# Opening rearranged, middle layers set up inside their own block, weight loads placed otherwise in the queue, last step's rows kept on chip

## The reference

```python
# 1: sliding-window attention (16 heads of 16, 4 key heads, window 64) and gelu feed-forward, 1024 wide
h = layernorm(x) * g1 + b1;  q, k, v = h @ Wq + bq, h @ Wk + bk, h @ Wv + bv;  q, k = rope(q), rope(k)
x = x + softmax(mask(q @ k.T / 4)) @ v @ Wo + bo
x = x + gelu((layernorm(x) * g2 + b2) @ Wf1 + bf1) @ Wf2 + bf2
# 2: two layers (8 heads of 64, windows of 128 and the window before)
for l in range(2):
    h = shift_token(x)                    # the right half of the columns comes from the row above
    q, k, v = split(h @ wqkv[l]);  q, k = xpos(l2norm(q) * qs[l]), xpos(l2norm(k) * ks[l])
    x = x + local_attention(8 * q, k, v) @ wo[l]
    h = layernorm(shift_token(x)) * lg[l] + lb[l]
    a, g = split(h @ w1[l] + b1[l]);  x = x + (a * gelu(g)) @ w2[l] + b2[l]
# 3: gated attention in chunks of 128: u * (relu(q @ k.T / sqrt(128) + bias)**2 @ v) @ o_w.T + o_b + x
# 4: linear layer with ternary weights
```

## Time and profile before

| | us |
|---|---|
| median of three runs (lowest, highest) | 2514.32 (2511.49, 2517.95) |
| the profiled execution's own time | 2506.83 |
| its span | 2505.0 |
| TensorE matmul busy | 2389.4 (95%) |
| VectorE busy | 1989.6 (79%) |
| ScalarE busy | 1570.0 (63%) |
| GpSimd busy | 1292.3 (52%) |

### The profile page before, as it was taken

One profiled execution on the slowest core, in us unless ns is written; L12 is line 12 of the kernel. 1 busy time (PEld: TensorE's weight loads), 2 busy tenths in 40 slices (PEclk: granted clock), 3 DMA queues, 4 the chain that ended last, 5 costly groups with the idle time before them and its releaser, 6 DMA issues. The chain is left out here.

```text
span 2505.0 us, 56134 instructions
## 1 busy us (share of the span) xinstructions
PE 2389.4 (95%) x19766; PEld 2160.8 (86%) x19766; DVE 1989.6 (79%) x6034; ACT 1570.0 (63%) x3630; POOL 1292.3 (52%) x1161
## 2 busy tenths in 40 slices
PE   7999999988899999999999999999879999999997
PEld 6899999977798998898888999999868888888886
DVE  6889989857889899899888999999567555775554
ACT  4788888755677887787777877877556113631111
POOL 3333233325766666767757667667247335743332
PEclk7999999997999999999999999999989999999998
DMA  2011221112222322323333223322343013311111
GB/s 80 21 34 38 71 86 59 35 43 82 91 82 89 98 82 87 98 85 111 105 102 98 89 80 98 92 77 92 100 155 107 28 34 101 97 59 34 34 34 43
DMA packets 223612, 189.75 MB, mean 76 GB/s; under 512 B 22372, under 2 KB 205800, under 8 KB 222312
## 3 DMA queue, kind: packets, MB, share of 16 engines
q1 hardware_dynamic: 204616, 176.52, 22.5%
q10 hardware_dynamic: 18720, 9.64, 1.4%
HBM read 90.60 MB, written 44.04 MB: 54 GB/s over the span
## 5 line engine op out<-in xcount | busy, mean ns | idle before, releaser
L1315 POOL TENSOR_TENSOR b_sb_probs<-b_sb_probs,b_sb_r_sum 128x512 f32<-128x512 f32 x256 | 269.3, 1072 | 330.8 <-DVE b_sb_r_sum L1568 330.8
L2078 POOL TENSOR_TENSOR c_kern_lo<-c_kern,c_kern_hi 128x512 fp32r<-128x512 f32 x128 | 178.2, 1392 | 302.3 <-ACT c_kern_hi L2167 302.3
L1399 ACT ACTIVATE b_sb_probs<-b_sb_probs,b_sb_neg_top,b_sb_r_norm 128x256 f32<-128x256 f32 x512 | 301.0, 590 | 2.1 <-DVE b_sb_neg_top L1535 1.2
L2167 ACT ACTIVATE c_kern_hi<-c_kern 128x512 fp32r<-128x512 f32 x128 | 80.9, 632 | 322.2 <-DVE c_kern L2277 322.2
L42 PE MATMUL psum<-b_sb_fT_lo,b_sb_w_hi 128*128 128x256 f32 x704 | 204.7, 291 | 1.4 <-DVE b_sb_fT_lo L1606 1.4
L42 PE MATMUL psum<-c_kern_lo,c_v_hi 128*128 128x512 f32 x512 | 199.7, 390 | 0.2
L44 PE MATMUL psum<-b_sb_fT_hi,b_sb_w_hi 128*128 128x256 f32 x704 | 199.6, 284 | 0.0
L44 PE MATMUL psum<-c_kern_hi,c_v_hi 128*128 128x512 f32 x512 | 199.5, 390 | 0.0
L43 PE MATMUL psum<-c_kern_hi,c_v_lo 128*128 128x512 f32 x512 | 199.3, 389 | 0.0
L43 PE MATMUL psum<-b_sb_fT_hi,b_sb_w_lo 128*128 128x256 f32 x704 | 199.3, 283 | 0.0
L1527 DVE CUSTOM_DVE_ANT_0 b_sb_probs<-psum,b_sb_mask 128x256 f32<-128x256 f32 x512 | 193.8, 416 | 2.1 <-PE psum L1712 1.6
(11 more groups left out here) (315 smaller groups left out, 8680.6 us busy)
## 6 DMA issues: line engine op xcount, KB each, us to landing
b_sb_kT_hi<-b_sb_kT_hi SPq DMA_DIRECT2D x64, 256.0 KB, 2.7
b_sb_kT_lo<-b_sb_kT_lo SPq DMA_DIRECT2D x64, 256.0 KB, 3.1
b_sb_v_prev<-b_sb_v_now SPq DMA_DIRECT2D x64, 256.0 KB, 2.5
Y<-b_sb_y SPq DMA_DIRECT2D x128, 128.0 KB, 2.5
b_sb_res<-Y SPq DMA_DIRECT2D x64, 128.0 KB, 2.9
b_sb_x_f<-Y SPq DMA_DIRECT2D x128, 64.0 KB, 2.1
b_sb_res_f<-Y SPq DMA_DIRECT2D x64, 128.0 KB, 2.5
U<-c_u_out SPq DMA_DIRECT2D x16, 512.0 KB, 4.6
```

What stands on the lines that cost most here:

```text
L1315: pool.tensor_tensor(p, p, r_sum[b][:, 2 * m:2 * m + 2, None].broadcast_to([P, 2, 2 * P]), ALU.mult)\
L1399: ins = act.activation(probs[b][:, n, :], probs[b][:, n, :], ACT.Exp, bias=neg_top[b][:, n:n + 1], scale=r_norm[b][:, h:h + 1], accum_out= ...
L2078: pool.tensor_tensor(kern_lo[i % RING][:], kern[i % RING][:], kern_hi[i % RING][:].bitcast(F32), ALU.subtract)\
L2167: act.activation(kern_hi[i % RING][:], kern[i % RING][:], ACT.Copy).then_inc(hi_ready, 1)
```

## The change

1. Opening of `layer_a`. The first row tile is loaded before the constants. The feed-forward weights leave `consts` for a part `weights_f` behind `load` 1. VectorE clears `qT` itself, with a semaphore of its own, and no engine waits for all constants at its start. In `project` the bias's matmul comes last and only it waits for the bias rows. `setup_a` is split: the weight's low part stays (`setup_w`), the bias rows move behind `norm` 1.
2. Passages. The last step's stores count on semaphores `a_handed` and `b_handed`, which live through the whole program. The end of the block does not wait for them; the next stage does, before its step 1 loads (SyncE and ScalarE in `layer_b`, SyncE in `layer_c`). They are cleared at the very end.
3. Opening of `layer_b`. The setup block is gone: its loads, splits and bias columns stand in the main lists, wqkv's parts first, w1's behind `turn_h` 1 and `spin_q` 0, wo's and w2's behind. The first six blocks of bias columns (`bias0`) are TensorE's first work, the other five come in step 0; the second layer's come in two pieces of five and six blocks, in steps 1 and 2 of TensorE's list, and `w1_early` is loaded after `rope` of step 1 and the splits. GpSimd clears fewer tiles, the keys' only in their left 128 columns.
4. `swap_f` 5 on SyncE moves from the ninth to the tenth shift and to the end of the turn.
5. In the last step `load_f` copies the rows from `y1` on chip, shifted by one partition for the right half, with the first row of that half from Y1.

```diff
 def layer_a(...):
-        "sp": [... ("load", 1, -1), ("consts", 0, -1),
+        "sp": [... ("load", 1, -1), ("weights_f", 0, -2), ("consts", 0, -1),
...
-                pool.memset(qT[b][:].bitcast(F32), 0.0).then_inc(consts_ready, 1)
...
-            dve.wait_ge(consts_ready, n_consts + 2)
+            for b in both:
+                dve.memset(qT[b][:].bitcast(F32), 0.0).then_inc(q_zeroed, 1)
...
-            pe.wait_ge(consts_ready, n_consts + 2)
...
             def project(t, b):
-                    pe.wait_ge(b_ready, 3)
+                    pe.wait_ge(consts_ready, n_consts + 2)
...
-                pe.matmul(out, e0[:], b_rows[:], start=True, stop=False)
                 for c in range(KC):
-                    ins = product3(..., False, c == KC - 1)
+                    product3(..., c == 0, False)
+                if t == 0:
+                    pe.wait_ge(b_ready, 3)
+                ins = pe.matmul(out, e0[:], b_rows[:], start=False, stop=True)
...
-            sp.wait_ge(y_stored, 16 * NT)
+            sp.wait_ge(y_stored, 16 * (NT - 1))
 def layer_b(...):
-        "pe": [... ("turn_p", 1, -1), ("bias", 0, 0), ("project_k", 1, 0), ...
+        "pe": [... ("down", 0, -4), ("bias", 2, -2), ..., ("up", 2, -3), ("bias", 1, -1), ..., ("project_v", 0, 0), ("bias", 0, 0), ...
-        "sp": [... ("down", 0, 8), ("swap_f", 5, 9), ("load_r", 0, 9), ... ("scores2", 0, 12)],
+        "sp": [... ("down", 0, 8), ("load_r", 0, 9), ... ("scores2", 0, 12), ("swap_f", 5, 10)],
...
-            setup = prepare.enter_context(nc.Block())
...
             def rope_(t, _):
                 if t == 1:
-                    sp.dma_start(w1_early[:], io["b2_w1"][1]).then_inc(early_in, 16)
+                    sp.wait_ge(a_handed, 32)
...
+                if t == 1:
+                    sp.wait_ge(raw_split, 7)
+                    ring.wait_full(sp, 0, ("bias", 0))
+                    sp.dma_start(w1_early[:], io["b2_w1"][1]).then_inc(early_in, 16)
...
             def load_f(t, b):
-                sp.wait_ge(stored[b], 16 * t + 16)
+                if t < steps - 1:
+                    sp.wait_ge(stored[b], 16 * t + 16)
...
+                if t == steps - 1:
+                    sp.wait_ge(stored[b], 16 * t)
+                    ring.wait_drained(sp, t, ("wo", b))
+                    sp.dma_start(x_f[:, b, 0:P], y1[b][:, 0:P]).then_inc(f_loaded[b], 16)
+                    sp.dma_start(x_f[1:P, b, P:D], y1[b][0:P - 1, P:D]).then_inc(f_loaded[b], 16)
+                    sp.dma_start(x_f[0:1, b, P:D], tile_rows(io["Y1"], t, b, slice(P, D), 1)[0:1, :]).then_inc(f_loaded[b], 16)
+                    return
...
         @block.scalar
+            for n in range(3):
+                act.activation(w_hi[:, :, qkv_cols(n)], w_raw0[:, :, qkv_cols(n)], ACT.Copy).then_inc(raw_hi, 1)
...
         @block.tensor
+            def shift(job, piece, cols, w, g):
+                out = ring.out(0, (job, piece), cols.stop - cols.start)
+                ring.wait_bank(pe, 0, (job, piece))
+                for n in range(cols.start, cols.stop):
+                    for c in range(KC):
+                        at = n - cols.start
+                        ins = pe.matmul(out[:, at:at + 1], w[:, c, n * P:(n + 1) * P], g[:, 1, c:c + 1], start=(c == 0),
+                                        stop=(c == KC - 1))
+                ring.written(0, ins, (job, piece))
+
+            shift("bias0", 0, slice(0, first), w1_raw0, gb)
...
+                    shift("bias", piece, early_cols[piece], w1_early, gb_next)
 def layer_c(...):
             def load(n):
+                if n == 1:
+                    sp.wait_ge(b_handed, 32)
```

More of the change, by code:

```diff
@@ L1076, in layer_b @@
         jobs.update(turn_f=["f"], up=["w"], down=["y"], bias=["bias"])
-        ring = Ring(sem, psum, f"{name}_ring", range(8), [(t, (job, b)) for stage, t, b in turns(order["pe"], steps)
+        ring = Ring(sem, psum, f"{name}_ring", range(8), [(0, ("bias0", 0))] + [(t, (job, b)) for stage, t, b in turns(order["pe"], steps)
                                                           if stage in jobs and (stage != "bias" or t == 0)
@@ L1267, in _ @@
                 sp.wait_ge(stored[b], 16 * steps)
-                sp.wait_ge(y2_stored[b], 16 * steps)
+                sp.wait_ge(y2_stored[b], 16 * (steps - 1))
         @block.gpsimd
         def _(pool):
-            pool.wait_ge(consts_ready, 9)
+            pool.memset(power[:], -0.5).then_inc(consts_ready, 1)
+            for b in both:
+                for part in (kT_hi[b], kT_lo[b]):
+                    pool.memset(part[:, :, 0:P].bitcast(F32), 0.0).then_inc(consts_ready, 1)
+                pool.memset(v_prev[b][:], 0.0).then_inc(consts_ready, 1)
+            pool.wait_ge(consts_ready, 7)
             def rope_(t, _):
+                if t == 0:
+                    pool.wait_ge(weights_in, 80)
                 pool.wait_ge(rope_loaded, 16 * t + 16)
@@ L1514, in spin_q, with add_bias @@
                 spin(t, b, 0, "q")
+                if (t, b) == (0, 0):
+                    for c in range(KC):
+                        dve.wait_ge(raw_hi, 4 + c)
+                        dve.scalar_tensor_tensor(out=w1_lo[:, c, :], in0=w1_raw0[:, c, :], scalar=gb[:, 0, c:c + 1],
+                                                 in1=w1_hi[:, c, :].bitcast(F32), op0=ALU.mult, op1=ALU.subtract)\
+                           .then_inc(raw_split, 1)
+            def add_bias(job, piece, out, of, n):
+                ring.wait_full(dve, 0, (job, piece))
+                ring.read(0, dve.tensor_tensor(out, ring.out(0, (job, piece), n), of, ALU.add), (job, piece))
+                ring.wait_drained(dve, 0, (job, piece))
             def turn_qk(t, b):
@@ L1629, in down, with bias @@
                 ring.read(t, dve.tensor_tensor(y2[:, b, :], ring.out(t, ("y", b), D), sum_f[:, b, :], ALU.add), ("y", b))
-            def bias(t, _):
-                if t == 0:
-                    ring.wait_full(dve, t, ("bias", 0))
-                    ring.read(t, dve.tensor_tensor(b1[:, 1, :], ring.out(t, ("bias", 0), n_in), b1[:, 1, :], ALU.add), ("bias", 0))
-                    ring.wait_drained(dve, t, ("bias", 0))
+            def bias(t, piece):
+                if t == 0 and piece == 0:
+                    dve.wait_ge(raw_hi, 6)
+                    dve.tensor_tensor(wo_lo[:], wo_raw0[:], wo_hi[:].bitcast(F32), ALU.subtract).then_inc(raw_split, 1)
+                    dve.wait_ge(raw_hi, 7)
+                    dve.tensor_tensor(w2_lo[:], w2_raw0[:], w2_hi[:].bitcast(F32), ALU.subtract).then_inc(raw_split, 1)
+                    add_bias("bias", 0, b1[:, 0, first:], b1_raw[:, first:], n_in - first)
+                    dve.sem_inc(bias_done, 1)
+                if t == 0 and piece > 0:
+                    dve.wait_ge(weights_in, 80)
+                    at = b1[:, 1, early_cols[piece]]
+                    add_bias("bias", piece, at, at, early_cols[piece].stop - early_cols[piece].start)
                     dve.sem_inc(early_done, 1)
```

205 lines of the change are left out of this document (97 added, 108 removed).

## The result

The changed kernel took 2507.58 us, median of 11 runs (2504.24 to 2513.38), against 2514.32 us of the kernel before (11 runs, 2511.16 to 2519.67): a ratio of 0.9972 with a 95% interval of 0.9961 to 0.9983, 6.7 us faster. The forecast was 12.2 us, 2502.1, in a range of 2489 to 2511. The profiled execution took 2505.77 us (span 2504.0, mean granted clock 0.973), only 1.1 us under that of before, which at 2506.83 was itself faster than all 11 runs.

What follows compares the result with a forecast made beforehand. TensorE was taken to bound the kernel, busy nearly everywhere at full clock, with gains only where it waits. Terms 3.9 + 1.7 + 3.5 + 0.7 + 1.0 + 1.4 = 12.2 us, from 2514.3 to 2502.1 us, range 2489 to 2511.

Steps and rivals of the forecast that it cites:

- Opening of the first stage: First stage's start: earlier normalisation, projection and second row tile, everything behind shifts; 3.9 us saved, between 1.5 and 4.5.
- The rival of the one-column matmuls: Bias groups inside dense work put TensorE at half clock, 13 us lost each: slower, 2541 us; chance 0.09.
- First passage: First to second stage: the block starts without waiting for the last store to land; 1.7 us saved, 1.6 to 2.0.
- Second passage: Passage to the last stage: SyncE goes on without waiting for the last store; 1.4 us saved, 1.2 to 1.6.
- Opening of the second stage: Second stage's start without setup block: earlier first scores, less clock and bias losses; net 3.5 us saved, 0 to 9.
- the 3.0 of the term: Second stage's first scores: loss set against the gain for TensorE at 1.2 GHz there, 3.0 us.
- The bias pieces: Second stage, steps 1 and 2: the next layer's 44 bias instructions as 20 and 24, 2.5 us taken as uncovered.
- Layer swap: Swap of layers: input weights issued a step earlier, so TensorE waits less; 0.7 us saved, 0 to 4.
- its upper case of 4 us: Layer swap: 4 us saved if the shorter gap also keeps the clock up.
- Last step: End of the second stage: rows copied on chip without waiting for the store; 1.0 us saved, 0 to 4.
- near 1790, and the term would be above 5: Last step: were the copy free of the queue, it would land in 1.7 us like a store.
- The rival "swallowed", 2506.5: Both stage openings: half of the 3.5 and 3.9 us comes back as VectorE's waits; 2506.5 us, chance 0.13.

Runs made afterwards that it cites:

- filler: Changed kernel plus twelve matmuls that compute nothing in TensorE's 2.15 us wait in the first stage's second step: 2486.4 us, 0.9976 of the kernel before.
- e_bopen: Kernel before with only the second stage's opening changed, the next layer's bias in two pieces included: 2495.3 us, ratio 1.0004.
- e_rows1: Kernel before with the last step's rows of the first sequence loaded ahead of the last stage's four early loads: 2487.1 us, ratio 0.9974.
- 2.7 in the second: Changed kernel timed again, unaltered, against the kernel before in a later session: 2491.6 us, ratio 0.9992.

## Why the prediction came out as it did

The direction and the range held in the first comparison; three steps were wrong, in size or sign, and a fourth, the layer swap, was sized too small. That the time still fell inside the range is in part luck.

*Opening of the first stage, 3.9 us.* Each step of the working came, and up to 53 us even 7.9 us, as the clock rose at 46.2 instead of 53.6. What I had not foreseen is that the clock then fell once more and took 7.2 us. What arrives at 115 us in the five traces of this opening without filler is 0.8, 0.5, 0.7, 5.2 and 5.0 us, 2.4 on average. The rival of the one-column matmuls named the kind of loss (a long stretch at half clock in a wholly busy engine) and the wrong cause: none of them stands at this place. That the 2.15 us wait starts it is likely and not shown: all six falls lie in it and none came where it was filled, but the traces with the filler differ from the others earlier. The Trainium skill (TensorE: Matmul & The Clock Gate, What's actually happening) says that activity releases the throttle: the traces with the filler agree, and the 20.5 us at half clock, without idle time behind the first 0.8 and spent on products of 17, 128 and 256 columns, do not. Why the old opening's equal wait passes in three traces of four stays open. (The new opening also holds a one-column copy on ScalarE, `warm`, that the description of the change leaves out; no run takes it alone.)

*First passage, 1.7 us:* 1.6. *Second passage, 1.4 us:* 1.1. Both by the next block beginning 2.1 us after the last issue.

*Opening of the second stage, 3.5 us.* The first failing step is in VectorE's chain. The first scores came 6.4 us earlier, not 7.7 to 9.0: they were forecast 27.0 us into the block and came at 29.6. VectorE's low parts of the weights were taken over at their price in the setup block, 3.3, 1.2 and 1.8 us. Here they stand in the main lists, beside GpSimd's work for keys and queries, and took 4.7, 1.6 and 2.6, which is 2.6 us more. (The 44 bias instructions, 9.3 us in the prediction, are 9.5 in the earlier trace rows; that hardly moves it.)

```profile
575.94 4.67 DVE L1519 SCALAR_TENSOR_TENSOR b_sb_w_lo<-b_raw_w,b_raw_gb,b_sb_w_hi 128x1408 fp32r<-128x1408 f32 x2
...
585.96 2.59 DVE L1650 TENSOR_TENSOR b_sb_w_lo<-b_raw_w,b_sb_w_hi 128x1536 fp32r<-128x1536 f32 x1
```

In all nine traces of the new opening they are longer, by 2.2 to 2.7 us together; why was not tried. The other two failing steps are those set against the gain. The clock was at half at the scores, as forecast, but filling the wait gives back some 1.2 us and not the 3.0 of the term. The bias pieces, of which I took 2.5 us as uncovered, cost their full 5.3 up to step 1's statistics: I had read "some 3 us to spare in each step" from a window that held TensorE's waits elsewhere in the step, and the groups stand where TensorE has none (idle for 0.0 us between 45 and 60 us into the block, and for 0.7 between 60 and 75). Kept at step 1's statistics: 0.9 us in this trace, nothing in the one of e_bopen, less than nothing against the old opening behind a new passage (115.9 and 116.0 against 117.4 to 118.8).

*Layer swap, 0.7 us:* TensorE's wait went from 4.38 to 3.63, 0.75. That was not all: of the row statistics, those at 1206.2 and 1331.8 lie three steps apart, 125.6 us, and in the changed kernel those at 1202.2 and 1325.3, 123.1 us. The five traces with `swap_f` 5 in its old place have 124.6 to 126.3 us here, eight of the nine with it moved 122.0 to 124.3 (the ninth, without the bias columns, 130.9): 2.0 us on average without the ninth. The forecast named this cause for its upper case of 4 us, the clock staying up: half clock behind the swap lasts 3.4 us instead of 6.9. But the other four traces with the old place have 3.4 there too, so what the move gives apart from TensorE's wait is open.

*Last step, 1.0 us.* The sign was wrong: TensorE waits 3.7 us longer. I had counted the third copy's 0.43 us of issue and taken the copies to be like the loads. The shifted one goes as if by one DMA engine, 3.0 us instead of under 0.5, twice, and the third was issued for 6.66 us. My estimate of what an unblocked load would give, "near 1790, and the term would be above 5", was borne out by e_rows1, 8.4 us for the change of order alone.

*Between these.* A step of the second stage takes 36.6 to 36.9 us or 37.3 to 37.6; in the longer ones TensorE stands idle for 0.81 us before products with the probabilities. The row names no releaser; VectorE's copies of the probabilities end 0.3 us before it, so they are the likely one:

```profile
1662.01 0.44 PE L1790 MATMUL psum<-b_sb_pT,b_sb_v_prev 128*64 128x128 f32 x4 [0.81 <-issue]
```

The trace of before has 13 such waits (of 0.75 to 0.9 us) between 600 and 1790 us, that of after 17, and those of the later sessions 0 to 11, as many in variants of the one kernel as of the other (up to 11 and up to 9). At 0.7 to 1.0 us each that is 3 to 4 us between the two profiles, which I don't put down to the change. Without it the parts come to 2.4 + 1.6 + 0.9 + 2.0 - 3.7 + 1.1 = 4.3 us by the traces, against 6.7 in the first comparison (4.3 to 9.8 by its interval) and 2.7 in the second (0.5 more to 4.7 less). The rival "swallowed", 2506.5, was closer than my forecast, but not by its mechanism: the clock, the bias columns and a copy swallowed most of the gain. VectorE took a part, by the longer low parts ahead of the first scores and not by the waits that the rival meant.

## What to carry to other kernels

A lead won in an opening has to be followed to the end of its stage: here 7 us of it went at half clock behind two microseconds of TensorE's idle time. A dozen matmuls that compute nothing in that wait gave 3.4 us (0.5 to 6.3), which is worth trying, but the traces don't settle how. Before a load is made shorter, look at what stands ahead of it in its queue: the order of two issues was worth 8 us, and the shortcut on chip less than nothing. Work moved onto a busy engine costs its full time unless the very place has a gap; a window's mean does not show that. And the duration of an operation in one place of the kernel need not hold in another.

## What the runs showed of the hardware

- A copy of 127 partitions of 512 bytes ran at 21 packets each half microsecond and a DMA share of 0.07; 128 partitions started in one half microsecond.
- The clock can be at half for 20.5 us while TensorE is busy without a gap for all but its first 0.7 to 0.8 us. The fall came 1.4 to 2.1 us into an idle time of 2.15 us in six traces, and lasted 20.5 us in four of them and 6.8 in two; in three traces with the same idle time it did not come.
- VectorE's low parts of w1, wo and w2 took 6.3 us together in the setup block and 8.6 to 9.0 in the main lists, beside GpSimd's products.
- The kernel before took 2514 us in the first comparison and 2495, 2494 and 2500 in the later sessions; the cause is not known. The second stage has from 0 to 17 of the 0.81 us waits, from trace to trace.
- Traces with the filler had the clock rise at 50.7 to 51.7 us in five of five, those with the new opening and no filler at 46.2 to 48.5. The filler runs only after that; I have no explanation.
